# First layer: four tiles of gathered rows are summed at another place in TensorE's order

## What is computed

```
xn = layernorm(x)
s  = recurrent cell over time(xn)            # gates f, i, o, z; c = f*c + i*z; h = o*tanh(LN(c))
g  = silu(tree(xn))
x  = x + s * g
```

```
logits = x @ W_in.T + b_in ; act = gelu(logits)       # for every node
current = root
for d in range(5):
    move    = argmax(act[current])                    # which of the 4 leaves
    current = child(current, move)
out = sum over the 6 visited nodes of  act[node] @ W_out[node]
```

## Time and profile before

| | us |
|---|---|
| median of 3 timed runs | 1525.26 (1523.7 to 1529.33) |
| the profiled execution's own time | 1539.31 |
| span of the profile, first to last instruction | 1537.5 |
| mean granted TensorE clock over the span | 0.92 |
| first layer, up to the table load of the next phase | 0 to 634.5 |

### The profile page before, as it was taken

One profiled execution on the slowest core, in us unless ns is written; L12 is line 12 of the kernel. 1 busy time (PEld: TensorE's weight loads), 2 busy tenths in 40 slices (PEclk: granted clock), 3 DMA queues, 4 the chain that ended last, 5 costly groups with the idle time before them and its releaser, 6 DMA issues.

```text
span 1537.5 us, 31027 instructions
## 1 busy us (share of the span) xinstructions
PE 1307.7 (85%) x9414; PEld 896.6 (58%) x9414; DVE 1241.8 (81%) x4011; ACT 1220.2 (79%) x3366; POOL 914.4 (59%) x1443
## 2 busy tenths in 40 slices
PE   8878888888788757899489999999999999999986
PEld 4546666655665534343256666666666666666665
DVE  3155968869696978378789999999999999999985
ACT  2256979788797978577488988988988989989985
POOL 0234454554546453057788778778778778778752
PEclk7888989898998867799699999999999999999998
DMA  3446686877769688369601101111101111101233
GB/s 109 156 174 202 206 313 219 285 251 246 261 206 321 223 327 279 86 177 304 244 22 37 41 14 42 44 45 33 45 12 44 44 44 34 37 18 45 68 103 105
DMA packets 152101, 210.17 MB, mean 137 GB/s; under 512 B 68224, under 2 KB 105216, under 8 KB 151808
## 3 DMA queue, kind: packets, MB, share of 16 engines
q0 software_dynamic: 36864, 134.76, 25.2%
q1 hardware_dynamic: 113952, 70.80, 16.6%
q10 hardware_dynamic: 1120, 2.64, 0.4%
HBM read 168.84 MB, written 26.74 MB: 127 GB/s over the span
## 4 chain that ended last, share of the span: by engine, by line
PE 25%; ACT 15%; issue 8%; POOL 2%; DVE 1%; ACTq 0%; DVEq 0%; POOLq 0%
ACT lo_s_ps L1801 5%; PE lo_qk_ps L1496 4%; PE lo_h_ps L1607 3%; PE lo_s_ps L1559 3%; PE lo_o_ps L1597 2%; ACT L1890 2%; PE lo_v_ps L1507 2%; ACT prepared_then_rounds L1861 1%; PE lo_s_ps L1546 1%; PE lo_h_ps L1619 1%; PE lo_ft_ps L1529 1%; ACT prepared_then_rounds L1809 1%; PE lo_o_ps L1579 1%; PE lo_ft_ps L1579 1%; ACT lo_V L1791 1%
## 5 line engine op out<-in xcount | busy, mean ns | idle before, releaser
L343 POOL DMA_INDIRECT wide<-in_table,l_idx x128 | 127.6, 997 | 183.2 <-PE l_acc L474 94.7
L1801 ACT ACTIVATE lo_s_ps<-lo_s_ps,lo_nmx,lo_rn 128x128 f32<-128x128 f32 x504 | 219.5, 440 | 2.1 <-DVE lo_nmx L2115 1.8
L343 POOL DMA_INDIRECT l_rows<-in_table,l_idx x128 | 130.0, 1016 | 150.2 <-DVE l_idx L842 86.8
L672 ACT ACTIVATE l_rows<-l_rows,l_act 128x128 f32<-128x128 f32 x512 | 153.1, 388 | 1.1
L672 ACT ACTIVATE wide<-wide,l_act 128x128 f32<-128x128 f32 x512 | 153.0, 387 | 0.8
L791 DVE CUSTOM_DVE_ANT_0 l_rows<-l_rows,xn_tok 128x128 f32<-128x128 f32 x512 | 143.7, 348 | 8.5 <-issue 5.3
L440 PEld LDWEIGHTS l_S<-pre,l_AT 128*128 128x128 f32 (+2 forms) x832 | 117.8, 209 | 51.9 <-ACT l_AT L657 31.4
L440 PE MATMUL l_S<-pre,l_AT 128*128 128x144 f32 (+3 forms) x832 | 129.8, 308 | 20.8 <-ACT l_AT L657 20.0
L791 DVE CUSTOM_DVE_ANT_0 wide<-wide,xn_tok 128x128 f32<-128x128 f32 x512 | 142.3, 347 | 4.5 <-DMA wide<-in_table,l_idx 4.5
L416 PE MATMUL l_log<-l_xT,top_in 128*128 128x512 f32 (+1 forms) x192 | 116.2, 698 | 23.0 <-ACT l_AT L657 21.9
L1990 POOL TENSOR_TENSOR lo_de_kS<-lo_de_S,lo_de_ops 128x384 f32<-128x384 f32 x128 | 128.6, 1005 | 10.0
(11 more groups left out here) (332 smaller groups left out, 3754.0 us busy)
## 6 DMA issues: line engine op xcount, KB each, us to landing
lo_VE<-lo_V SPq DMA_DIRECT2D x64, 128.0 KB, 2.4
scratch_ops<-prepared_then_rounds SPq DMA_DIRECT2D x4, 1792.0 KB, 7.1
lo_de_ops<-scratch_ops SPq DMA_DIRECT2D x16, 448.0 KB, 4.2
lo_de_qo<-scratch_qo SPq DMA_DIRECT2D x16, 256.0 KB, 4.6
scratch_qo<-prepared_then_rounds SPq DMA_DIRECT2D x7, 512.0 KB, 8.7
x_tok<-in_x SPq DMA_DIRECT2D x8, 256.0 KB, 5.3
wide<-in_table,l_idx POOLq DMA_INDIRECT x128
l_rows<-in_table,l_idx POOLq DMA_INDIRECT x128
```

The lines of the kernel that those rows point to most:

```text
L343: pool.indirect_dma_start(rows[L][:, r % SLOTS, p, :], None, a[f"table{L}"], bass.IndirectOffsetOnAxis(ap=at[:, p:p + 1], axis=0)).then_in ...
L672: ins = act.activation(z, z, ACT.Copy, scale=act_of(L, r)[:, k:k + 1])
L1801: ins = act.activation(here, here, ACT.Exp, scale=rn[:, v % 2, j, 2 * k + e:2 * k + e + 1], bias=nmx[:, j, e, k:k + 1], accum_out=sums[:, ...
```

## The change

Only TensorE's order differs. In the order of one pass of the loop over `g`: level-4 tile 1 is summed between `weigh` 8 and `weigh` 9 instead of behind `weigh(g - 1, 0)`; level-5 tile 2 behind `logits(g - 1, 0)` instead of behind level-4 tile 1; level-4 tile 2 behind gate 1 instead of in front of gate 2; level-4 tile 3 behind level-5 tile 0 of its group and in front of `weigh(g - 1, 2)` instead of behind gate 3. No instruction is added or taken away, and the other four engines have the same instructions in the same order.

```diff
@@ -545,6 +545,9 @@
                 if on(g - 2):
                     weigh(g - 2, 7)
                     weigh(g - 2, 8)
+                if on(g - 3):
+                    spread_rows(4, GT * (g - 3) + 1)
+                if on(g - 2):
                     weigh(g - 2, 9)
                     logits(g - 2, 10)
                     penalty(g - 2, 10)
@@ -552,6 +555,8 @@
                     penalty(g - 2, 11)
                 if on(g - 1):
                     logits(g - 1, 0)
+                if on(g - 4):
+                    spread_rows(5, GT * (g - 4) + 2)
                 if on(g - 2):
                     weigh(g - 2, 10)
                 if on(g - 1):
@@ -560,12 +565,10 @@
                     weigh(g - 2, 11)
                 if on(g - 1):
                     weigh(g - 1, 0)
-                if on(g - 3):
-                    spread_rows(4, GT * (g - 3) + 1)
-                if on(g - 4):
-                    spread_rows(5, GT * (g - 4) + 2)
                 if on(g - 2):
                     gate(g - 2, 1)
+                if on(g - 3):
+                    spread_rows(4, GT * (g - 3) + 2)
                 if on(g - 4):
                     spread_rows(5, GT * (g - 4) + 3)
                 if on(g - 1):
@@ -579,8 +582,6 @@
                     turn_f(g - 4)
                 if on(g - 1):
                     logits(g - 1, 3)
-                if on(g - 3):
-                    spread_rows(4, GT * (g - 3) + 2)
                 if on(g - 2):
                     gate(g - 2, 2)
                 if on(g - 1):
@@ -588,6 +589,7 @@
                     penalty(g - 1, 3)
                 if on(g - 3):
                     spread_rows(5, GT * (g - 3) + 0)
+                    spread_rows(4, GT * (g - 3) + 3)
                 if on(g - 1):
                     weigh(g - 1, 2)
                     weigh(g - 1, 3)
@@ -595,8 +597,6 @@
                     logits(g - 1, 4)
                 if on(g - 2):
                     gate(g - 2, 3)
-                if on(g - 3):
-                    spread_rows(4, GT * (g - 3) + 3)
                 if on(g):
                     turn_x(g)
             z(NG - 1)
```

## The result

| | before | after |
|---|---|---|
| median of 16 timed runs each, us | 1528.72 (1523.7 to 1535.8) | 1539.69 (1528.34 to 1543.8) |
| the profiled execution's own time, us | 1539.31 | 1540.18 |
| first layer, up to the table load of the next phase | 634.5 | 637.6 |

The ratio is 1.0065, 95% interval 1.0047 to 1.0083: **0.65% slower**, about 10 us. Forecast were 12 us less. The profiled execution of the kernel before lies above all 16 of its timed runs, the changed kernel's lies among them; so the two traces differ by 0.9 us only, and a comparison of them shows where time moved, not the whole 10 us.

A forecast was written before the change was run, and what follows sets the result against it. It took the first layer to be bound by waits on TensorE's completions, delayed during long gather runs. Savings of 10.8 + 1.4 = 12.2 us from 1539.3 gave 1527.1; less 14.05 to the median, 1513 us, range 1495 to 1541.

The forecast's parts named there:

- the first term of the sum: Shorter waits in front of `choose(h, 2)`: 1.8 us a group over six groups, 10.8 us saved (bounds -12 and +20.4).
- the last step of the sum: From profiled execution to timed median: 14.05 us subtracted, taking 1527.1 to 1513 us.
- the ring: First layer's 65.7 us period: no engine is full, so a cycle of waits between engines sets it.
- held news: TensorE's completions reach others late while long gather runs load DMA engines, 1.5 to 2 us after the run's end.
- Point 1: Level-4 tile 1 and level-5 tile 2 go into TensorE's holes: cost 0, or 1.9 us a group without cover.
- Point 2: Level-4 tile 2 summed earlier, freeing 3 us of TensorE in front of gate 2: by itself worth 0.
- Point 3: Level-4 tile 3 in front of level 2's weighings: 0 to 0.7 us of loss.
- Point 4: Earlier sums let gather runs shift and join, up to twenty; `choose(h, 2)` gains 1.8 us a group, upper bound 3.4.
- Point 5: Layer's end: tile 28's sum done near 593.3 instead of 594.7, 1.4 us saved (bounds 0 and 2.76).
- The slower one: Rival: joined run holds news for `choose(h, 1)`; 2 us a group lost, 1536 us; chance 0.28.
- the hold is a matter of the profiled execution: Version of the no-change rival: timed runs lack the hold, 1524 us; a quarter of that rival's 0.27 chance.
- The holds go: Rival: spread-out gathers hold nothing, period falls to 60.2 us, time 1491 us; chance 0.09.

The follow-up runs named there:

- sb: Kernel before, but from each level's fourth tile on a gather brings 16 bytes of a row instead of 4112; 1535.64 us, ratio 1.0009.
- spb: Kernel before, gathers issued by SyncE as plain DMAs of the same size from fixed table places, GpSimd idle in the first layer; 1455.16 us, ratio 0.9526.
- p42: Kernel before with only level-4 tile 2 moved, plus eight GpSimd buffer fills (pauses of 3 us) behind each tile's gathers; 1529.85 us, ratio 0.9935.
- m41: Kernel before with only level-4 tile 1 moved; 1526.18 us, ratio 0.9986.
- m52: Kernel before with only level-5 tile 2 moved; 1527.49 us, ratio 1.0004.
- m4152: Kernel before with only level-4 tile 1 and level-5 tile 2 moved; 1551.03 us, ratio 1.0091.
- sp42: Kernel before with only level-4 tile 2 moved and gathers issued by SyncE as plain DMAs; 1467.52 us, ratio 0.9610 against the kernel before.
- spa: The whole change with gathers issued by SyncE as plain DMAs; 1453.84 us, ratio 0.9514 against the kernel before.
- m43: Kernel before with only level-4 tile 3 moved; 1533.16 us, ratio 1.0047.
- m42: Kernel before with only level-4 tile 2 moved, behind gate 1; 1573.10 us, ratio 1.0299.
- pa4: The whole change plus four GpSimd buffer fills (pauses of 1.5 us) behind each tile's gathers; 1477.86 us, ratio 0.9611 against the kernel before.

## Why the prediction was wrong

The direction was wrong and the time 26.7 us too low, though inside the range. The step that failed is the first term of the sum, 10.8 us for a shorter hold in front of `choose(h, 2)`. The hold did get shorter, by 22.2 us, but the six periods together gained 2.0 only: VectorE lost the rest between `choose(h, 2)` and the next `choose(h, 3)`, for which the sum had no term of its own beyond halving an upper bound, and the startup, which it left out, lost 4.6. Of the 26.7 us, 14.05 come from the last step of the sum, 12.2 from its terms, and about 0.4 is the 0.9 between the two profiled executions less the 0.5 by which the second stands above its median.

- *What bounds the kernel.* That the ring is made of TensorE's held news was right: with it gone the kernel takes 72 us less. The sentence that failed is "while a long run of gathers loads the DMA engines". The load is innocent (sb), GpSimd's unbroken issuing is not (spb, p42). From the rows shown the two could not be told apart, since a run of gathers is both; the share of 1.02 was taken for the cause because it stood beside the hold.
- *Point 1*, both tiles into holes at no cost: right for each alone (m41, m52), wrong for the two together (m4152, 14 us) beside GpSimd's gathers.
- *Point 2*, "by itself this is worth 0": the worst price of a single move. By itself it costs 46 us. I priced TensorE's side of the move and left GpSimd's to point 4. Some 12 of the 46 are TensorE's order (sp42 against spb), which the step had at 0. In the whole change this doesn't show: spa is no slower than spb.
- *Point 3*, 0 to 0.7 us a group, 4.2 over six: m43 measured 6.
- *Point 4*, the runs come earlier, join, and the hold in front of `choose(h, 2)` shrinks. They came 5 to 6 us earlier but did not join: where up to twenty gathers were foretold, there are eight, and GpSimd's waits for level-4 sums rose from 74.0 to 84.5 us instead of falling far below. The hold shrank by 22.2 us where I counted 10.8, so the term was not too large at its own place. Other places lost: in front of `choose(h, 3)` 8.4 us, in the second group's `choose(h, 1)` 9.2, by VectorE's halts inside its dot products some 14 (10.5, 9.2 and 4.1 where there were 5.3, 4.6 and none listed). What remains over six periods is 2.0 us. The step treated the hold as a place in one period that can be shortened while the rest stays as it is. Why the rest did not stay, the traces don't settle. The startup, where the runs of 4 and 8 became twelve, wasn't looked at, and lost 4.6.
- *Point 5*, 1.4 us at the layer's end: wrong. The sum of tile 28 now waits for its own scaling, as said, but ends at 594.5 and not near 593.3; the gather starts at 595.29 instead of 595.66. VectorE's wait for its rows fell from 2.76 to 1.41 us mostly because VectorE itself came 1.2 us later, and the stretch behind the last scans took 1.1 us longer.
- *From the profiled execution to the median*: I subtracted 14.05 us as if a profile cost that much. The changed kernel's profiled execution lies among its timed runs. The kernel before has a spread of 12 us over 16 runs, and in other sessions its timed runs reach from 1521.3 to 1543.4 us, so 1539.31 is a long execution of it and needs no cost of the profiler. With that step at 0 the forecast would have been 1527 and read as no change.
- *The rivals.* The slower one put its price at 2 us a group and its place at `choose(h, 1)`; 1536 was nearest to the result of all, by luck: the waits in front of `choose(h, 1)` fell a little (28.6 to 25.3 us), the stretch up to it took 3.8 us less over five periods, and no joined run stood there. The loss lay behind `choose(h, 2)` and in the startup. Alone, level-4 tile 2 is this rival as described (m42), at 46 us. That the hold is a matter of the profiled execution is refuted: the timed runs, too, gain 72 us when GpSimd is silent. By the Trainium skill's overflow rule (NOTIFIC — the notification-queue block, section on overflow), taken alone, they would have gained nothing. *The holds go* (1491) was right of the mechanism but not of this change; pa4, which takes them away, measures 1477.86.

## What to carry to other kernels

Where an engine's wait ends only when GpSimd's run of indirect DMAs does, break the run before anything else is tuned: a pause of about 1.5 us behind every four, by work that nobody waits for, was worth 3.9% here together with the change's order, while four careful moves of TensorE's work were worth nothing or less. A move that frees a buffer earlier must be priced on the queue that waits for the buffer, startup included, and moves that are free alone must be run together. Before a profile is compared with a median, look whether that execution lies among the timed ones.

## What the runs showed of the hardware that I had not expected

- TensorE's completion news can be held while GpSimd issues indirect DMAs without a pause: 3.7 and 6.6 us in runs of 8, 11.5 us in the run of 16. In the holds read here it then comes 1.5 to 3 us behind the last one, but one hold of about 3 us in m42 ended within the run. 0.05 or 0.74 of DMA share makes no difference, nor do a quarter of the rows.
- SyncE's plain DMAs of the same size at 289 GB/s hold nothing (0.04 us from the weighing's end to VectorE's start in spb). Whether plain DMAs issued by GpSimd would hold news was not tried.
- GpSimd's fills of its own buffer hold nothing either, and 1.44 us of them between groups of four gathers are enough (pa4, again 0.04 us), although behind longer runs the news took 1.5 to 3 us.
- While its news is held TensorE runs dry and its granted clock falls. In m42, over the 15 us up to the end of its 11.5 us hold and the 2 us behind it, it was 0.70 and 0.50, the latter the 1.2 GHz level:

```profile
268.00:283.00 15.00, 6.96 (x32) 4.96 (x32) 1.38 (x2) 10.30 (x35) 9.32 (x10) 0.70 1.02 397
283.00:285.00 2.00, 0.13 (x4) 0.13 (x6) 1.67 (x8) 0.00 (x0) 0.00 (x0) 0.50 0.86 343
```

- Why news is held at all, whether in GpSimd's descriptor writing or in a path for semaphores that it shares with the other engines, is not shown by these runs.
